# Linear attention with post-norm and a feed-forward block on eight cores: five rows of merged heads transposed by TensorE, up-projection filler from step 40

## The reference

```python
def attention(x, Wq, Wk, Wv, Wo, bo, proj):           # 16 heads of 64, 256 random features
    Q, K, V = heads(x @ Wq.T) / 8, heads(x @ Wk.T) / 8, heads(x @ Wv.T)
    def phi(y):
        yw = einsum('bhtd,hmd->bhtm', y, proj)
        yw = yw - max(yw, axis=-1)
        return (exp(yw) * exp(-0.5 * sum(y * y)) + 1e-6) / sqrt(256)
    KV   = einsum('bhtm,bhtd->bhmd', phi(K), V)
    Ksum = sum over t of phi(K)
    num  = einsum('bhtm,bhmd->bhtd', phi(Q), KV)
    den  = einsum('bhtm,bhm->bht', phi(Q), Ksum) + 1e-6
    return merge_heads(num / den) @ Wo.T + bo
def ffn(y): return relu(y @ W1 + b1) @ W2 + b2         # 1024 -> 4096 -> 1024
x = layernorm(x + attention(x))
x = layernorm(x + ffn(x))
```

## Time and profile before

| | us |
|---|---|
| timed runs | 1597.15, 1600.81, 1621.22; median 1600.81 |
| profiled execution | 1598.1 |
| its span (slowest core, number 5) | 1596.6 |
| spans of the eight cores | 1589.9 to 1596.6 |
| mean granted TensorE clock | 0.992 to 0.993 |
| TensorE busy in the span | 1549.2 |
| ScalarE, VectorE, GpSimd busy | 729.8, 679.4, 555.2 |

### The profile page before, as it was taken

One profiled execution on the slowest core, in us unless ns is written; L12 is line 12 of the kernel. 1 busy time (PEld: TensorE's weight loads), 2 busy tenths in 40 slices (PEclk: granted clock), 3 DMA queues, 4 the chain that ended last, 5 costly groups with the idle time before them and its releaser, 6 DMA issues.

```text
span 1596.6 us, 28140 instructions; the slowest of 8 cores (1589.9 to 1596.6 us)
## 1 busy us (share of the span) xinstructions
PE 1549.2 (97%) x9816; PEld 722.8 (45%) x9816; DVE 679.4 (43%) x1385; ACT 729.8 (46%) x1663; POOL 555.2 (35%) x471
## 2 busy tenths in 40 slices
PE   8999999997898899999999999999999999999998
PEld 3455554553444344444444444444444444444443
DVE  4788888887774444444444444100011111111111
ACT  3577777776674555556655565343311111111111
POOL 4466666661354543444434433000021111111110
PEclk9999999999999999999999999999999999999999
DMA  9576678319996758476584757267674414433110
GB/s 182 135 123 107 105 107 131 66 34 226 209 211 126 197 130 198 123 171 160 126 199 132 146 156 188 79 141 149 126 250 159 150 61 165 165 97 128 60 53 40
DMA packets 260202, 219.95 MB, mean 138 GB/s; under 512 B 206048, under 2 KB 206560, under 8 KB 256608
## 3 DMA queue, kind: packets, MB, share of 16 engines
q1 hardware_dynamic: 249664, 185.65, 43.9%
q0 software_dynamic: 10400, 32.51, 13.9%
HBM read 137.38 MB, written 68.16 MB: 129 GB/s over the span
## 4 chain that ended last, share of the span: by engine, by line
PE 90%; SPq 2%; DVE 2%; DMA 2%; ACT 2%; issue 1%; POOL 0%; DVEq 0%; ACTq 0%; POOLq 0%
PE bk L73 53%; PE ps L73 37%; SPq L68 2%; DVE maxa L80 1%; ACT eq L74 1%; DMA wk0f<-WkT 1%; DMA eta<-eq 1%; ACT e L74 1%; DVE r L79 0%; DMA r<-x 0%; SPq L62 0%; DVE bia L79 0%; POOL r L77 0%; DVE mrg L77 0%; DVE qk L76 0%
## 5 line engine op out<-in xcount | busy, mean ns | idle before, releaser
L80 DVE TENSOR_REDUCE maxa<-ps 128x4 f32<-128x1024 f32 x256 | 311.8, 1218 | 119.5 <-PE ps L73 119.1
L74 ACT ACTIVATE eq<-ps,bia 128x256 bf16<-128x256 f32 x512 | 200.7, 477 | 218.7 <-DVE bia L79 107.1
L74 ACT ACTIVATE e<-ps,bia 128x256 bf16<-128x256 f32 x512 | 202.3, 487 | 90.0 <-DVE bia L79 85.3
L73 PE MATMUL bk<-rt,w 128*128 128x512 bf16 x1032 | 240.9, 379 | 0.0
L73 PE MATMUL ps<-rt,w 128*128 128x512 bf16 x1016 | 238.6, 381 | 0.0
L73 PE MATMUL ps<-w,ht 128*128 128x512 bf16 x1024 | 223.6, 379 | 0.0
L73 PE MATMUL bk<-w,ht 128*128 128x512 bf16 x1024 | 223.6, 379 | 0.0
L74 ACT ACTIVATE jnk<-out,nmu 128x1024 bf16<-128x1024 f32 x32 | 36.7, 1148 | 383.6 <-DVE nmu L78 383.6
L77 POOL TENSOR_TENSOR out<-rn,b2b 128x1024 f32<-128x1024 bf16 x32 | 68.2, 2135 | 361.4 <-DMA out<-out 334.4
L78 POOL TENSOR_SCALAR eq<-eq 128x1024 bf16<-128x1024 bf16 x88 | 91.8, 1043 | 243.6 <-ACT eq L74 243.4
L78 POOL TENSOR_SCALAR e<-e 128x1024 bf16<-128x1024 bf16 x128 | 133.5, 1043 | 106.3 <-ACT e L74 101.4
(11 more groups left out here) (85 smaller groups left out, 1443.9 us busy)
## 6 DMA issues: line engine op xcount, KB each, us to landing
h_d<-hts SPq DMA_DIRECT2D x112, 256.0 KB, 2.6
ht<-h_d SPq DMA_DIRECT2D x14, 2048.0 KB, 15.5
r<-x SPq DMA_DIRECT2D x32, 512.0 KB, 4.8
out<-out SPq DMA_DIRECT2D x32, 512.0 KB, 2.9
x_d<-xb SPq DMA_DIRECT2D x8, 1024.0 KB, 12.2
xb<-x_d SPq DMA_DIRECT2D x8, 1024.0 KB, 8.0
r1n_d<-r1n SPq DMA_DIRECT2D x32, 256.0 KB, 3.0
w<-W POOLq DMA_DIRECT2D x4, 2048.0 KB, 16.9
```

Source lines behind the costliest of these rows:

```text
L73: "matmul": lambda g, *a, **k: g.matmul(*a, **k),
L74: "activation": lambda g, *a, **k: g.activation(*a, **k),
L80: "reduce_max": lambda g, *a, **k: g.reduce_max(*a, **k),
```

## The change

- Rows whose wo comes before `S_UP` (`by_pe`: rows 32 to 36) have their merged heads transposed on TensorE: eight transposes of 128x128 against an identity `IDN` into one PSUM bank, read as bfloat16, and one ScalarE copy to `MGT`. The others keep the DMA transpose. The identity is a new input, loaded on GpSimd's queue in step 6.
- `S_UP` falls from 42 to 40. `w_step` is three steps behind the features instead of four for rows below 38; rows 38 and 39 both fall into step 41. Steps 40 and 41 hold 2 and 4 up-projections; steps 64 and 65 keep 12.
- In steps 33 to 39 a group runs in the order features, numerators, one long sum: a projection in groups 0 and 1 (before: 0 and 2), wo in groups 2 and 3 (before: 1 and 3), and the transposes behind the projection in group 0. These sums, the transposes and the constants' rows take banks 4 and 5 in turn.
- bo is added for rows from 39 on in group 0 of the step with their wo, before it at the end of the step ahead.
- `load_rt` for the first tile is issued from step 39, group 1, to step 40, group 0 (before: step 39, group 2, to step 40, group 3). W2 is loaded after 0, 11, 22 and 33 of the remaining 42 up-projections (before: 8, 20, 32 and 44 of 56).

```diff
+    idn_h = din("idn", [128, 128])
+    IDN = small("idn_sb", [128, 128], BF16, 256)
-    S_UP = 42
+    S_UP = 40
     def w_step(r):
-        return {S_UP - 3: S_UP, S_UP - 2: S_UP + 1, S_UP - 1: S_UP + 1}.get(
-            r, r + 4 if r < S_UP else r + 2)
+        return {S_UP - 2: S_UP + 1, S_UP - 1: S_UP + 1}.get(r, r + 3 if r < S_UP else r + 2)
+    def by_pe(r):
+        return w_step(r) < S_UP
+    def transpose_pe(r, b):
+        pe.wait(mrg_ready[r], idn_ready, *free[b])
+        t = BK[b].bitcast(BF16).rearrange("p (c t) -> p c t", c=8)
+        for c in range(8):
+            tok = pe.do("transpose", t[:, c, :], MRG[r % 2][:, c * 128:(c + 1) * 128], IDN[:, :],
+                        mark=(c == 7))
+        act.wait(tok, mgt_done.get(r - 2))
+        tm[r] = act.do("copy", out=MGT[r % 2][:, :, :], in_=t, mark=True)
+        free[b] = (tm[r],)
+    turn45 = [0]
+    def bank45():
+        turn45[0] += 1
+        return 4 + turn45[0] % 2
-        return {0: 2 * su, (1 if su == 3 and nt > 10 else 2): 2 * su + 1}
+        return {0: 2 * su, (1 if 32 <= s < S_UP or (su == 3 and nt > 9) else 2): 2 * su + 1}
         if s == 6:
+            idn_ready = load(pool, "s_idn", IDN[:, :], idn_h[:, :])
-    ups = {S_UP: 4, S_UP + 1: 4, 64: 12, 65: 12}
+    ups = {S_UP: (0, 0, 1, 1), S_UP + 1: (1,) * 4, 64: (3,) * 4, 65: (3,) * 4}
-    rt_at = {(39, 2): [(0, 0)], (40, 0): [(0, 1)], (40, 1): [(0, 2)], (40, 3): [(0, 3)]}
+    rt_at = {(39, 1): [(0, 0)], (39, 2): [(0, 1)], (39, 3): [(0, 2)], (40, 0): [(0, 3)]}
         for g in range(4):
-            if s < S_UP:
+            if s == 32:
                 begin(s, g)
             elif s < 64:
-                features(s, g, 0)
+                features(s, g, g % 2 if s < S_UP else 0)
             spill_h()
+            if g == 0:
+                for r in wos:
+                    if r >= S_UP - 1:
+                        add_bo(r)
             if 0 <= 4 * (s - 33) + g - 1 < 4:
-                eps_row(4 * (s - 33) + g - 1, 5)
+                eps_row(4 * (s - 33) + g - 1, bank45())
             if s < S_UP:
                 ...
-                if g % 2 == 1:
-                    for r in wos:
-                        wo(r, g // 2, 5)
                 for r in nums:
                     num(r, g)
+                if s > 32 and g in chunks(s):
+                    project(s, g, bank45())
+                for r in wos:
+                    if g == 0:
+                        transpose_pe(r, bank45())
+                    if g > 1:
+                        wo(r, g - 2, bank45())
                 ...
             else:
-                nu = ups.get(s, 8) // 4
+                nu = ups.get(s, (2,) * 4)[g]
             ...
             if g == 3:
-                for r in range(32, 64):
-                    if w_step(r) == s + 1 and r in x_ready:
+                for r in range(32, S_UP - 1):
+                    if w_step(r) == s + 1:
                         add_bo(r)
-                if nums:
+                if nums and not by_pe(nums[-1]):
                     transpose_m(nums[-1])
-            if (s, g) == (39, 2):
+            if (s, g) == (39, 1):
                 rt_place[0] = xb_done[10]
     while up_n[0] < 256:
-        if up_n[0] - n0 in (8, 20, 32, 44):
+        if up_n[0] - n0 in (0, 11, 22, 33):
             pool.wait(up_tok[0])
-            load_w2((up_n[0] - n0 - 8) // 12)
+            load_w2((up_n[0] - n0) // 11)
```

## The result

The changed kernel takes 1612.68 us (median of five runs, 1609.42 to 1614.45) against 1600.81: ratio 1.0091, 95% interval 1.0067 to 1.0116. It is 0.9% slower, where 0.6% faster was forecast, and lies 12 us above the forecast's range.

A forecast was written before the change was run, and what follows sets the result against it. TensorE, busy 97% of 1596.6 us, was taken to bound the kernel, with 29.5 us winnable at the handover. 3.7 - 4.0 + 5.2 + 1.7 = 6.6 us won from 1598.1 gives 1591.5, stated as 1591; range 1580 to 1601.

The forecast's parts named there:

- Tail: Up-projections behind the loop: fourteen sums move out at equal cost; W2's last quarter has 25.9 us against a 16.9 landing.
- steps 37 to 39: Second projection waits 0.9 a step for its bank, plus 0.45 of transposes: 3 x 1.35 = 4.0 us lost.
- The cost of the bo addition: From step 40, bo's addition in wo's own step: POOL's 2.35 us stays covered by about 3 to 6 us.
- steps 34 to 36: DMA still decides; step 36 waits until 405.8 with a cold clock; step 37 starts at 415, 3.7 us won.
- The three long gaps: TensorE gaps of 3.79, 4.10 and 5.24 us in steps 34, 36 and 44; no handover gap over 3 us expected.
- The eight transposes: On TensorE, a row's eight overlapping transposes take 0.45 us, between 0.26 and 0.64; 2.2 us for five rows.
- Steps 40 to 44: Filler from step 40: of 12.2 us of idle time and cold clock, 7.0 remains, so 5.2 won.
- The relief: Rival: five fewer DMA transposes empty the queue so step 36 does not stop; 8.4 more won, 1583; chance 0.20.
- the transposes did overlap: Rival that TensorE's transposes do not overlap: 6.6 us more, 1598; chance 0.09.
- the handover: Rival: step 40 stalls as long as steps 42 to 44 did, the 5.2 are not won, 1597; chance 0.09.
- The slower rival: Second projection waits in each of steps 37 to 39: 14.4 us more, 1606; slower from 2.2 more a step; chance 0.12.
- no more than 2% would show: Whole kernel: 29.5 us ceiling, 1.8%, nearly rules out a gain over 2%; under 1569 given 0.04, over 1633 given 0.03.

The follow-up runs named there:

- experiment 1: Changed kernel with W2's four loads after 8, 17, 26 and 35 of the remaining 42 up-projections instead of 0, 11, 22 and 33: 1600.05 us, ratio 1.0004.
- experiment 2: Kernel before the change, with only W2's loads moved to after 0, 12, 24 and 36 of its 56 remaining up-projections: 1611.4 us, ratio 1.0081.
- experiment 4: On top of experiment 1, bo is not added for rows 32 to 38: 1594.44 us, ratio 0.9982.
- experiment 5: On top of experiment 1, bo is added in wo's step and held on GpSimd until group 0's bias is done: 1594.1 us, 0.9971 by the medians.
- experiment 8: On top of experiment 5, the TensorE transposes stand at the head of group 0, ahead of the step's features: 1593.8 us, ratio 0.9970.
- experiment 3: Changed kernel with W2 loaded after 4, 14, 24 and 34 of the 42 up-projections: 1599.9 us, ratio 1.0005.
- experiment 7: On top of experiment 1, rows 32 to 36 have their merged heads transposed by DMA again: 1598.7 us, ratio on record 0.9953 (0.9861 to 1.0046).

## Why the prediction was wrong, step by step

**The step that failed** is *Tail*: "TensorE works there without gaps" and "Hidden, with 9 us to spare". It asked whether W2 arrives before it is read, which it does, and not what the load meets when it starts. The parts were in the prediction's own account: 14 sums fewer in the tail and a first load after 0 sums instead of 8 put a 2 MB load onto the last four `RT` transposes. Costed at nothing, it took 12.5 us (experiment 1; 13 in experiment 2, where the same move of the load was made in the kernel before).

**Mis-sized: steps 37 to 39.** The forecast was 0.9 of wait and 0.45 of transposes a step. Measured: a wait of 0.72 for the copy of the projection, 0.54 for the transposes, and 1.60 + 0.37 for the numerators' bank, which the sum had no term for. The three steps lasted 42.1 us (417.0 to 459.1) instead of 3 x 12.4 (11.1 as before and the 1.35 of the forecast), so 4.9 more were lost than forecast. The cost of the bo addition was asked only of those who wait for its result; that GpSimd holds up VectorE while it runs was not considered (experiments 4 and 5).

**Mis-sized: steps 34 to 36.** Step 37 began 63.5 us behind step 32, not 61.2. The prediction let TensorE wait in step 36 for the copy of the projection, behind exponentials that wait for the DMA until 403.6, with a cold clock after it. Measured: these exponentials start at 404.46, released by VectorE and not by the DMA, as the bias ahead of them took 1.95 us beside the bo addition. TensorE waits first for the numerators' bank and then for the copy, at a granted clock of 1.00:

```profile
405.24 0.27 PE L73 MATMUL bk<-crow,onesr 1*128 1x260 bf16 x1 [1.77 <-DVE mrg L77]
...
409.78 1.89 PE L73 MATMUL bk<-xb,wq 128*128 128x512 bf16 x8 [0.85 <-ACT qk L75]
```

The cold clock came in steps 34 and 35 instead (granted 0.82, sums of eight of 3.40 and 3.60 us), among short waits for `mrg` (1.09, 1.66) and for KV. No experiment separates what steps 32 to 35 lost.

**Right.** The three long gaps went. The eight transposes overlap: from their first start to that of the next group 0.54 us, within the bounds of 0.26 to 0.64, at a granted clock of 1.00 (0.80 in the first of the five rows, where the granted clock is 0.82). By the Trainium skill's 275 ns (TensorE: Matmul & The Clock Gate, Part 4: PE-mode transpose) eight would take, as an estimate, 2.2 us; 0.54 for eight is 68 ns each, so the trace doesn't agree with that figure as a cost of each. The granted clock did not fall beside them, among ordinary matmuls; no run shows a longer stretch of transposes alone. Steps 40 to 44 keep 6.1 us of gaps and 1.2 of cold clock, 7.3, where 7.0 were forecast, so 4.9 of the 5.2 us were won.

**The account** on the slowest core: forecast 1591.5, + 2.3 (steps 32 to 36) + 4.9 (37 to 39) + 0.3 (40 to 44) + 14.4 (tail) = 1613.4; the profiled execution took 1612.6. The tail counts 14.4 here, as on this core, and 12.5 in experiment 1, where another core is the slowest.

**The rivals.** None was what happened. The relief did not go further; the transposes did overlap; the handover did not merely move, although its idle time did, into short waits. The slower rival was nearest: a wait in each of steps 37 to 39, but for the bias and not for the projection's copy, and 1.6 us instead of the 2.2 from which it would have decided. The top of the range, which ends at 1601, held the change without its tail's collision (experiment 1: 1600.05); without the bias' wait as well the time came within 3 us of the forecast (experiments 5 and 8: 1594). That no more than 2% would show was right; the sign was not.

**What stays open.** Which resource the W2 load and the transposes contend for was not separated: that the load changes the data type and goes through GpSimd's queue, or its size alone, would give the same picture. That ScalarE goes on right behind the landing of W2 on every core suggests that the stores are held up until then, but not how; in experiment 3 the stores beside the load land before it. In experiment 7 the interval is too wide to say whether the DMA transposes are a little better.

## What to carry to other kernels

A load that moves in time has two questions: whether it arrives before it is read, and which transfers are in flight when it starts; list the queue's neighbours at the new place, for here it was the small stores among them that stopped the engines. And an instruction on GpSimd is paid not only by those who wait for its result: look whether a VectorE instruction with two SBUF inputs stretches to the same end, and put it where VectorE is in a long instruction that reads PSUM (in experiment 5 the maxima took 1.22 us beside the addition, and 1.21 to 1.23 without it). When a relief brings nothing, compare the *sum* of idle time by stage; the long gaps may be gone and the short ones have taken their place.

## What the runs showed of the hardware that was not expected

- A VectorE instruction of 0.16 us took 1.79 beside a GpSimd addition of 2.34, up to the end of the latter within 0.03 us; it took 0.86 to 1.0 beside GpSimd's square of 1.04.
- A 2 MB load started among four DMA transposes raised their issue on SP's queue from 5.5 to 12.3 us on the slowest core (5.6 to 18.7 on the eight), their landing from 4.8 to 11.1, and that of 256 KB stores behind them from 2.6 to 14.8. Started 3.3 us after the last issue, it stopped no engine, and no store on the slowest core took over 8.8 us (8.5 in the kernel before).
- Eight TensorE transposes of 128x128, each shown with 0.22 us, followed each other in 0.54 us, at a granted clock of 1.00 among other matmuls.
